# Loops of VectorE and ScalarE over eight steps instead of two, and the end of a Runge-Kutta step written in another order

## The reference

```python
def derivative(q, p, drive):
    dq = q - q ** 3 / 3.0 - p + drive + tanh(q) @ coupling.T + bias
    dp = EPSILON * (q + ALPHA - BETA * p)
    return dq, dp
# q1 = q, q2 = q + DT/2 dq1, q3 = q + DT/2 dq2, q4 = q + DT dq3
# q_next = clip(q + DT/6 (dq1 + 2 dq2 + 2 dq3 + dq4), -20, 20); p_next likewise
```

## Time and profile before

| | |
|---|---|
| median of 3 runs | 5927.5 us |
| the profiled execution | 5931.63 us |
| its span | 5929.8 us |
| granted clock of TensorE, share | 0.995 |
| VectorE busy | 5526.4 us, 93% |
| TensorE matmuls busy | 4508.3 us, 76% |
| ScalarE busy | 2595.9 us, 44% |

### The profile page before, as it was taken

The page is one execution under the profiler, slowest core; times in us unless marked ns, Lnnn a source line. Parts: engine busy times, 40 slices in busy tenths (PEclk is TensorE's granted clock), DMA queues, the critical chain, the costliest instruction groups (busy, mean ns, idle before and its releaser), DMA issues.

```text
span 5929.8 us, 592455 instructions
## 1 busy us (share of the span) xinstructions
PE 4508.3 (76%) x263627; PEld 3814.4 (64%) x263627; DVE 5526.4 (93%) x31560; ACT 2595.9 (44%) x12040; POOL 5.6 (0%) x16
## 2 busy tenths in 40 slices
PE   7887777777777777777777777777777777777777
PEld 3446666666666666666666666666666666666666
DVE  6569999999999999999999999999999999999999
ACT  3334444444444444444444444444444444444444
POOL 0000000000000000000000000000000000000000
PEclk9999999999999999999999999999999999999999
DMA  5100000000000000000000000000000000000000
GB/s 211 45 16 0 0 7 0 7 0 7 0 0 7 0 7 0 7 0 0 7 0 7 0 7 0 0 7 0 7 0 7 0 0 7 0 7 0 7 0 7
DMA packets 11597, 57.06 MB, mean 10 GB/s; under 512 B 2616, under 2 KB 2616, under 8 KB 8512
## 3 DMA queue, kind: packets, MB, share of 16 engines
q1 hardware_dynamic: 11056, 55.84, 2.4%
q10 hardware_dynamic: 528, 1.05, 0.0%
HBM read 40.11 MB, written 16.78 MB: 10 GB/s over the span
## 4 chain that ended last, share of the span: by engine, by line
DVE 44%; PE 34%; issue 11%; ACT 10%; DMA 1%; DVEq 0%; SPq 0%; ACTq 0%
PE ps L619 29%; DVE xb L661 23%; DVE turned_sums L811 10%; ACT xb L437 7%; DVE tanh_parts L661 4%; ACT tanh_parts L443 3%; DVE xb L936 2%; DVE xb L834 2%; PE ps L508 1%; DVE xb L932 1%; DVE xb L927 1%; PE ps L563 1%; PE ps L526 1%; PE ps L552 1%; PE ps L542 1%
## 5 line engine op out<-in xcount | busy, mean ns | idle before, releaser
L619 PE MATMUL ps<-coup,tanh_parts 128*16 128x96 f16 (+1 forms) x262272 | 4159.4, 219 | 1345.7 <-DVE tanh_parts L661 680.6
L619 PEld LDWEIGHTS ps<-coup,tanh_parts 128*16 128x16 f16 x262272 | 3653.2, 89 | 1852.4 <-issue 863.9
L437 ACT ACTIVATE xb<-xb 128x24 f32<-128x24 f32 (+1 forms) x4098 | 940.7, 230 | 2968.7 <-DVE xb L661 2958.5
L661 DVE SCALAR_TENSOR_TENSOR xb<-xb 128x64 f32<-128x64 f32 x11267 | 2198.2, 214 | 17.7 <-issue 0.2
L661 DVE SCALAR_TENSOR_TENSOR xb<-turned_sums,step_scale,xb 128x64 f32<-128x64 f32 (+2 forms) x6145 | 1601.2, 261 | 16.2
L811 DVE STREAM_TRANSPOSE turned_sums<-ps 128x96 f32<-128x96 f32 (+1 forms) x4096 | 1284.2, 314 | 142.2 <-PE ps L619 67.3
L661 DVE SCALAR_TENSOR_TENSOR tanh_parts<-xb,tanh_parts 128x24 f16<-128x24 f32 (+1 forms) x4098 | 712.8, 174 | 49.9
L443 ACT ACTIVATE tanh_parts<-xb 128x24 f16<-128x24 f32 (+1 forms) x2050 | 470.9, 230 | 64.5
L481 ACT ACTIVATE xb<-xb 128x64 f32<-128x64 f32 x2048 | 498.8, 244 | 0.0
L834 DVE SCALAR_TENSOR_TENSOR xb<-xb 128x64 f32<-128x64 f32 x2049 | 445.6, 217 | 0.1
L455 ACT ACTIVATE tanh_parts<-xb 128x24 f16<-128x24 f32 (+1 forms) x2048 | 357.4, 221 | 32.1
(11 more groups left out here) (68 smaller groups left out, 792.7 us busy)
## 6 DMA issues: line engine op xcount, KB each, us to landing
xb<-in_x SPq DMA_DIRECT2D x8, 2048.0 KB, 7.9
drive<-in_x_pt SPq DMA_DIRECT2D x8, 2048.0 KB, 24.6
out_pt<-drive SPq DMA_DIRECT2D x16, 1024.0 KB, 4.5
drive<-in_coupling_t SPq DMA_DIRECT2D x8, 512.0 KB, 11.5
mask_v<-in_cond SPq DMA_DIRECT2D x8, 132.0 KB
probs<-in_wo ACTq DMA_DIRECT2D x1, 1024.0 KB, 5.5
w_qkv<-in_wq SPq DMA_DIRECT2D x1, 64.0 KB, 3.8
w_qkv<-in_wk SPq DMA_DIRECT2D x1, 64.0 KB, 5.2
```

Source lines behind the costliest of these rows:

```text
L437: nc.scalar.activation(cols(tanh_sb, CHUNKS[j]), cols(q, CHUNKS[j]), ACT.Tanh)\
L619: last = nc.tensor.matmul(product(s, j)[SQ * g:SQ * g + ROWS, :], tanh_parts[:, s % 2, k, :], coup[:, k, part, g, n0:n1, :].rearrange("p c ...
L661: return V.scalar_tensor_tensor(out=out, in0=a, scalar=factor, in1=c, op0=ALU.mult, op1=op1)
```

## The change

`UNROLLED` goes from 2 to 8, for VectorE and ScalarE alike (TensorE's loop has its own constant and stays). In stage 3 `p_next` is gone and `clip_p` stands in its place, `drive_less_p` goes ahead of `clip_q`, `cubic_of(0)` goes ahead of `with_first_part`, and `g0_of` between `with_first_part` and `base_of`. In stage 2 `p_sum_q3` goes ahead of the tail's sums and `p_next` is made between `cubic_of` and `base_of`. Three semaphores and six waits per step are added for these orders.

```diff
-UNROLLED = 2
+UNROLLED = 8
...
-            def base_of(stage, made):
+            def base_of(stage, made, linear=None):
                 dve.wait_ge(cubic_ready, made)
+                if linear is not None:
+                    dve.wait_ge(zero_ready, linear)
...
             def z_of_first(now=None):
                 if now is not None:
                     dve.wait_ge(drive_p_ready, now)
+                    dve.wait_ge(clipped, steps_until(now))
...
             def p_sum_q3():
-                axpy(p_sum[3][:, :], q_st[3][:, :], 1 / P_ALL, p_sum[2][:, :])
-            def p_next():
-                axpy(p_raw[:, :], p_sum[3][:, :], DT / 6 * EPS * P_ALL, p_st[:, :])
-            def clip_p():
+                axpy(p_sum[3][:, :], q_st[3][:, :], 1 / P_ALL, p_sum[2][:, :]).then_inc(p_sum_ready, STAGES)
+            def p_next(now):
+                dve.wait_ge(p_sum_ready, now)
+                axpy(p_raw[:, :], p_sum[3][:, :], DT / 6 * EPS * P_ALL, p_st[:, :]).then_inc(p_raw_ready, STAGES)
+            def clip_p(now):
+                dve.wait_ge(p_raw_ready, now)
...
                 if s == 3:
-                    p_next()
+                    clip_p(now)
...
                 if s == 3:
-                    clip_p()
+                    drive_less_p(now)
                     clip_q(made)
-                    drive_less_p(now)
...
                 if s == 2:
                     forecast_first(made)
+                    p_sum_q3()
                     dve.wait_ge(z_rest_ready, now)
                     with_first_part(3, z_first_part, z_rest)
                     cubic_of(3, made)
-                    p_sum_q3()
+                    p_next(now)
                     base_of(3, made)
                 if s == 3:
                     z_of_first(now).then_inc(z_ready, STAGES)
+                    cubic_of(0, made)
+                    dve.wait_ge(z_ready, now)
+                    with_first_part(0, z_first_part, z).then_inc(zero_ready, STAGES)
                     g0_of()
-                    dve.wait_ge(z_ready, now)
-                    with_first_part(0, z_first_part, z)
-                    cubic_of(0, made)
-                    base_of(0, made)
+                    base_of(0, made, now)
```

More of the change, by code:

```diff
@@ L265, in build @@
         p_ready = sem("p_ready")
+        p_sum_ready = sem("p_sum_ready")
+        p_raw_ready = sem("p_raw_ready")
+        zero_ready = sem("zero_ready")
         q_share_ready = sem("q_share_ready")
```

## The result

The changed kernel takes 6169.5 us (median of 4 runs, 6160.36 to 6177.63) against 5928.1 for the kernel before: ratio 1.041, 95% interval 1.039 to 1.043. It is 4% slower where 1.5% was forecast, and lies above the stated range. The profiled execution has a span of 6158.6 us, 228.8 more than the 5929.8 of before.

What follows compares the result with a forecast made beforehand. The prediction took a ring of TensorE and VectorE, neither alone, to bound the kernel. From 5931.6 us, - 46 (order) - 51 (removed branches) + 186 (remaining branches) = 6020.6, less 4.1 to the median: 6016 us, range 5833 to 6095.

Steps and rivals of the forecast that it cites:

- What bounds the kernel: Whole step: a ring through TensorE and VectorE, neither alone; VectorE makes stage 3 lose 0.11 us a step.
- Reordering, stage 3: VectorE's new order takes stage 3 from 2.74 to 2.63 us; -46 us over 512 steps with stages 2 and 0.
- The rival of lone waits: Stage 3's tail: waits that are instructions of their own eat the order's gain, 6062 us; within the forecast's case of 0.50.
- Stage 2: VectorE's stage 2, where `p_next` comes in: grows by 0.01 us a step, by up to 0.08.
- stage 0: The stage after stage 3: begins 0.11 us earlier, can't keep all of its 2.62 us, +0.01 us a step.
- The branch, removed ones: VectorE's backward branches, 254 now and 62 after: removing today's cost of 254 x 0.20 us gives -51 us.
- The branch, what is left of it: VectorE's 62 remaining branches: the 41 KB body misses its buffer, 3.0 us each, +186 us, between +12 and +260.
- the range's upper end: Whole kernel: 6095 us, for a branch of 4.2 us.
- its sign of five packets a pass: VectorE's loop: about five instruction packets of 8 KB each pass, some 320 in all, where none were.
- the buffer that holds the body: Rival, VectorE's loop: the body fits and the branch stays at 0.20 us, 5843 us; chance 0.23.
- the cheap fetch: Rival, VectorE's branch: it misses but costs little, 5880 us at 0.8 us a branch; chance 0.18.
- ScalarE's miss: Rival, ScalarE's loop: its 264 instructions miss too, 1.5 us show at each of 62 branches, 6109 us; chance 0.09.

Runs made afterwards that it cites:

- four_fast: The changed kernel with both loops over four steps, `z_ready` and `zero_ready` counted by one per step, two pairs of waits turned: 5859.7 us, ratio 0.988.
- two_shift: The changed kernel with both loops over two steps and 16 empty instructions ahead of VectorE's loop: 5901.2 us, ratio 0.9946.
- loops4_only: The kernel before, its order kept, with both loops over four steps: 5907.6 us, ratio 0.996.
- scalar8: The changed kernel with VectorE's loop over two steps as before and ScalarE's over eight: 5927.6 us, ratio 0.9992.
- order_only: The changed kernel with both loops over two steps as before: 5926.7 us, ratio 0.9988.
- loops8_only: The kernel before, its order kept, with both loops over eight steps: 6148.6 us, ratio 1.036.
- four_shift: The changed kernel with both loops over four steps and 16 empty instructions ahead of VectorE's loop: 6383.6 us, ratio 1.077.
- warm8: The changed kernel with 24 more TensorE matmuls of 160 columns behind each stage's products, into a bank nobody reads: 6120.0 us, ratio 1.032.
- sixteen: The changed kernel with both loops over sixteen steps: 6022.3 us, ratio 1.016.

## Why the prediction was wrong

**What bounds the kernel** held: the ring of TensorE and VectorE, and 0.11 us of VectorE in stage 3. `four_fast` takes just these 0.11 us away: stage 3 goes from 2.744 in the kernel before to 2.635.

**Reordering, stage 3**: -46 us forecast, -31 measured (`two_shift` alone, 31.5). The layout was right up to `rest_of` and then ran 0.04, 0.06 and 0.07 us late: `z_of_first` at 1.81, `with_first_part` at 2.15, `base_of` at 2.54 us from the transpose, where 1.77, 2.09 and 2.47 stood. The timeline of a stage 3 of the changed kernel that has no boundary:

```profile
2342.60 0.28 DVE L814 STREAM_TRANSPOSE turned_sums<-ps 128x96 f32<-128x96 f32 x1
...
2344.24 0.20 DVE L664 SCALAR_TENSOR_TENSOR tanh_parts<-xb,tanh_parts 128x40 f16<-128x40 f32 x1
2344.41 0.23 DVE L664 SCALAR_TENSOR_TENSOR xb<-xb 128x64 f32<-128x64 f32 x1
2344.55 0.22 DVE L837 SCALAR_TENSOR_TENSOR xb<-xb 128x64 f32<-128x64 f32 x1
2344.75 0.28 DVE L664 SCALAR_TENSOR_TENSOR xb<-turned_sums,step_scale,xb 128x64 f32<-128x64 f32 x1
2344.95 0.41 DVE L664 SCALAR_TENSOR_TENSOR xb<-xb 128x64 f32<-128x64 f32 x2
2345.28 0.28 DVE L814 STREAM_TRANSPOSE turned_sums<-ps 128x96 f32<-128x96 f32 x1
```

`z_of_first` starts at 2344.41, 0.17 us behind a `rest_of` whose place is 0.12 long. Two waits stand between them, and they seem to take the sequencer some time although both are over; `four_fast` keeps both, and the 0.17 us. I had priced a lone wait only by its delay behind the result. The rival of lone waits was thus right in part. **Stage 2** kept its 2.64 us and **stage 0** its 2.62; the 0.01 each was not there (stage 0's came in `four_fast`, once stage 3 was short).

**The branch, removed ones**: 254 x 0.20 = 51, and `loops4_only` confirms the price of one (127 x 0.20 = 25 expected, 25 measured).

**The branch, what is left of it** is the step that failed, in size. That the body doesn't fit was right. The wait itself was put at 3.0 us and measures 2.69. But the term, 62 x 3.0 = 186 us, was only the wait; a pass pays 2.69 + 1.37 + 0.95 = 5.01 us, 311 in all. Two sentences of the forecast carry the omission, which put both other parts at nothing. "In line order the fetch runs ahead" is true for the data and false for the time: an entry into a block that starts the fetch of the next takes VectorE's sequencer up to 0.37 us, where one that starts none takes 0.1. And "TensorE, ScalarE and the next stage all wait" stopped short of the granted clock: TensorE had a gap of 0.61 to 0.67 us a stage in the trace before (0.82 at the branch), and the 3.3 us that it has at a branch now are followed by half its clock in 55 of 62 passes. With the three sizes of the table the forecast would have been 5928 - 31 - 51 + 311 = 6157. The sizes come from the profiled executions, and these explain the other 12 us: that of the changed kernel is the quickest of its four, 9 us below their median (its granted clock was 0.976, the others' 0.973 to 0.975), and that of the kernel before was 3.5 us above its median.

Two smaller slips of the forecast: its sign of five packets a pass was low, since the body touches six blocks and one more is fetched ahead (seven), and the range's upper end, a branch of 4.2 us, adds up to 6091 us, not 6095.

Of the rivals, the buffer that holds the body and the cheap fetch are refuted by the packets and by 2.69 us; ScalarE's miss, at eight steps, by `scalar8`. The packet itself is short indeed: in the pass shown it runs from 2312.67 to 2313.22. But it starts 0.9 us behind VectorE's last work, and VectorE's branch row follows only 1.4 us after it has landed. The Trainium skill's 32 KiB ("Runtime: NRT & Kernel Launch", "Instruction fetch mechanics") agrees with the runs. Its blocks of 16 KiB, two of them, don't: VectorE is refilled by 8 KB, and three blocks can be looped over.

The gap at a boundary has two parts. The boundary behind the 63rd instruction lies ahead of the same `base_of` in `order_only` and in the changed kernel: it costs 0.10 us in the first, where no fetch starts, and 0.37 in the second, where one does. Why the start of a fetch holds VectorE's sequencer stays open, and so does what sets how often TensorE's clock falls behind a stall.

## What to carry to other kernels

Before a loop is unrolled, count its instructions on each engine and see in which blocks of code they lie; on VectorE a body within three blocks of 128 was refilled in no pass, the wait that a fourth brings costs as much per pass as thirteen backward branches that hit, and sixteen instructions ahead of the loop can decide it. An instruction packet inside a loop is the sign to look for, and the price of a stall on one engine includes what the clock of TensorE does after it. In a chain of dependent sums on VectorE, a user whose wait rides on it starts some 0.07 us earlier than one whose wait stands alone (0.03 us behind the end of the result against 0.10 to 0.11), so counting by one, where the wait value allows it, is a change of its own.

## What the runs showed of the hardware

- A backward branch of VectorE costs 0.20 us with its target in the buffer and 2.69 us without (2.84 in `loops8_only` and `four_shift`).
- Entering the next block of 128 instructions costs VectorE up to 0.10 us, and up to 0.37 where it starts the fetch of the block behind; the packet starts 0.67 us behind the late instruction.
- Moving a loop by 16 places made it 25 us faster (`two_shift`) or 496 us slower (`four_shift`).
- TensorE's granted clock fell to 0.50 behind 55 of 62 branches when it idled 3.3 us at each in the mean (3.42 in the pass shown), behind 25 of 62 in `warm8` with 2.9 us, and behind 10 of 30 in `sixteen` with 3.4 us. In the kernel before, with a gap of 0.61 to 0.82 us in every stage, it did not fall from 500 to 5900 us.
- ScalarE's body of some 260 instructions caused no fetch in 64 passes, nor did TensorE's 520 in 1024. ScalarE's of some 515 missed in every pass of `sixteen`.
